# Two homes for the mixture outputs, one GpSimd loop over pairs of blocks, and a second mixture that finishes its chunk pairs one by one

## The chip, the cores and the metric

One Trainium2 chip, one of its cores. The metric is the device time of one execution in microseconds (us), as the median of a few runs.

## The reference

Two layers work on 2048 tokens of width 256 (two sequences of 1024). Each layer is a cross-attention to 154 context rows, and then a mixture of 8 experts of which every token uses its best two:

```python
x = x + attention0(layernorm(x), ctx)          # 16 heads
x = x + mixture0(layernorm(x))                 # silu(x@wg) * (x@wu) @ wd, inner width 1024
x = x + attention1(layernorm(x), ctx, phi)     # one head
x = x + mixture1(layernorm(x))                 # gelu(x@W1a) * (x@W1b) @ W2, inner width 512
# mixture: per token the two largest gate logits, softmax over them as shares;
# mixture1 keeps at most 640 (token, expert) pairs for one expert, the rest is dropped
```

## The kernel before

The program is written by hand, one instruction stream for each engine, with semaphores between them. In each mixture the tokens are first sorted by expert: GpSimd scatters the normalised rows (and two shares, the token's number and the expert, all in one row) into a buffer `rows` in HBM, with a region for each expert. Each region is padded with rows whose token number lies out of range. Then `experts(l)` runs on TensorE, ScalarE and VectorE (l.n is 0 or 1 for the two mixtures). It walks over **blocks** of 256 rows of one expert; a last block of an expert with at most 128 rows is done at half width (`width` P instead of BLK), which I call a half block. Which blocks belong to which expert is read at run time from a small `table` that `count(l)` on VectorE fills.

A number with about 22 bits is carried as two fp16 parts, `hi` and `lo`, so each product takes three matmuls. The inner width is cut into **chunks** of 128 columns and two chunks form a **pair**; the first mixture has 4 pairs for each block, the second has 2. For block g:

- TensorE (`one_block`) computes gate and up of each pair into PSUM banks, transposes block g+1 (`turn_block`), waits until the outputs of block g-1 have left their banks (semaphore `_y`), and then computes the outputs (L685 is the helper `mm` of all matmuls): first all products with `h_hi`, then all with `h_lo`. For the second mixture a full block has 48 matmuls for gate and up, 8 transposes (L933) and 24 for the outputs; a half block has 48 at half the columns, 8, and 12.
- ScalarE computes the activation of the gate (L1267), casts the product to its high part `h_hi` (L1271), starts the load of block g+2 (`load`, L1253, into the one `x_raw`), and at the end waits for the output products and for the semaphore `_added`, and writes the outputs times their share from PSUM to `yb` (L1280).
- VectorE multiplies activation and up (`h32`, L1804), takes the low part `h_lo` (L1809), and in `turned(g+1)` copies the transposed block from PSUM to `xbT` (L1783) and works out its shares and token numbers, `carried` (L1786 to L1790).
- GpSimd (`add_results`) goes over the experts and in each over its blocks. For a block it copies the token numbers to `row_to` (L571), waits for `yb`, issues two indirect DMAs of 128 rows that add `yb` to the sums in HBM (L575), waits until they have landed (L580), and raises `_added`.

There is one `yb`, so the outputs of block g leave PSUM only when the addition of block g-1 has landed; and the ScalarE stream stands at this wait, with the activations of block g+1 behind it. There is one `x_raw`; its next load waits for `carried`, which reads the ends of its rows.

The weights of a coming expert are split beside the blocks: SyncE loads a chunk of 1024 columns, ScalarE makes its high part (`high_part`, L1129) and VectorE its low part (`low_part`, L1405). In the second mixture there are 3 such chunks for each expert, all beside the first block of the expert two before; I call such a block a splitting block. At what step of the block each is done stands in

```python
l.beside     = (([0], [1], [2], [3, 4], [5]), ([0], [1, 2], []))[n]   # ScalarE
l.low_beside = (([0], [1], [2], [3], [4, 5]), ([0], [], [1, 2]))[n]   # VectorE
```

After the first mixture, SyncE waits for `_added` of all blocks and loads the sums as the new x. At the end of the second it waits in the same way, and the program is over when all engines have come to their ends.

## Time and profile before

| | |
|---|---|
| median of 3 runs | 883.97 us (883.52 to 884.15) |
| span of the profiled execution | 889.0 us, 5.0 over the median |
| TensorE matmuls busy | 700.3 us, 79% of the span |
| VectorE / ScalarE / GpSimd busy | 547.8 / 403.1 / 302.8 us |
| mean granted TensorE clock | 0.889 of full speed |
| chain that ended last | TensorE 48%, VectorE 18%, "issue" 11%, ScalarE 9%, GpSimd 5%, DMA 5% |

For the profiled execution the page gives the span from its first to its last instruction and no other time of its own. The profiler records one execution, and all durations below are from it. Times in the rows are us from the start of the span. The clock is a share of full speed (1.00 is 2.4 GHz, 0.50 is 1.2 GHz). "Idle before <-releaser" is how long the engine stood before the instruction and what released it.

### The profile page before, as it was taken

To read this page: it belongs to the slowest core of one execution; us is meant where nothing else is said; L and a number is where in the kernel's file an instruction comes from. 1 tells how busy PE (TensorE), PEld (TensorE's weight loads), DVE (VectorE), ACT (ScalarE), POOL (GpSimd) and SP (SyncE) were. 2 spreads that over 40 slices of the span, in tenths; PEclk is the share of its full clock that TensorE was granted. 3 is DMA by queue.
4 is the path that set the end of the run, shared out by engine and by line. 5 is a ranking of instruction groups with operands and counts; after the bars stand their busy time and mean duration, and the time that the engine had idled before them with its cause. 6 is when DMAs were issued, how large, how long until landed. Compare 5 with 4: busy or idle time off the path is not lost.

```text
span 889.0 us, 19049 instructions
## 1 busy us (share of the span) xinstructions
PE 700.3 (79%) x6278; PEld 550.1 (62%) x6278; DVE 547.8 (62%) x1322; ACT 403.1 (45%) x720; POOL 302.8 (34%) x306
## 2 busy tenths in 40 slices
PE   5476796989564799999999899996862098898981
PEld 4232454555354688888897798895531087777771
DVE  7768576887836545647556656547696446566441
ACT  1135466576513434646545555442552044546331
POOL 7505301416337422222121131232167414334342
PEclk9689799989776799999999999997875599999996
DMA  4562300601524542536344643425022555464332
GB/s 140 118 141 51 59 2 24 180 24 49 153 81 151 185 129 36 165 51 171 78 126 98 170 112 101 107 39 179 25 101 95 174 170 131 115 147 114 63 55 40
DMA packets 68418, 92.24 MB, mean 104 GB/s; under 512 B 14442, under 2 KB 54435, under 8 KB 68348
## 3 DMA queue, kind: packets, MB, share of 16 engines
q1 hardware_dynamic: 41788, 63.37, 24.1%
q0 software_dynamic: 14592, 16.24, 10.6%
q10 hardware_dynamic: 11968, 11.72, 5.3%
q8 instruction: 42, 0.69, 0.3%
q14 instruction: 28, 0.23, 0.1%
HBM read 64.21 MB, written 29.87 MB: 106 GB/s over the span
## 4 chain that ended last, share of the span: by engine, by line
PE 48%; DVE 18%; issue 11%; ACT 9%; POOL 5%; DMA 5%; ACTq 2%; another core or an unknown queue 1%; DVEq 0%; POOLq 0%; SPq 0%
PE ps L685 45%; POOL rows L631 3%; DVE probs L1726 3%; DVE mx L1591 2%; DMA out_x<-keys,row_to 2%; DVE keys L1804 2%; DMA probs<-rows 2%; ACT probs L1189 1%; ACT probs L1271 1%; ACT expo L1186 1%; DVE keys L1783 1%; ACT probs L1267 1%; PE ps L933 1%; DVE stats L1383 1%; ACTq L1252 1%
## 5 line engine op out<-in xcount | busy, mean ns | idle before, releaser
L1804 DVE TENSOR_TENSOR keys<-probs,ps 128x512 f32<-128x512 f32 x122 | 82.8, 687 | 177.3 <-ACT probs L1267 86.3
L685 PE MATMUL ps<-keys,slot 128*128 128x256 f16 (+1 forms) x1440 | 146.5, 263 | 5.4 <-DVE keys L1783 2.7
L685 PE MATMUL ps<-keys,probs 128*128 128x256 f16 (+1 forms) x1488 | 139.5, 255 | 5.1 <-DVE probs L1405 3.7
L685 PEld LDWEIGHTS ps<-keys,slot 128*128 128x128 f16 x1440 | 127.8, 99 | 22.8 <-issue 5.4
L685 PEld LDWEIGHTS ps<-keys,probs 128*128 128x128 f16 x1488 | 124.2, 98 | 19.0 <-issue 7.2
L575 POOL DMA_INDIRECT attended<-keys,row_to x42 | 67.2, 1601 | 166.0 <-ACT keys L1280 142.2
L1267 ACT ACTIVATE probs<-ps 128x512 f32<-128x512 f32 x122 | 71.4, 598 | 65.9 <-PE ps L685 63.7
L1280 ACT ACTIVATE keys<-ps,carried 128x256 f32<-128x256 f32 x80 | 33.5, 470 | 117.9 <-POOLq L580 41.6
L1809 DVE TENSOR_TENSOR probs<-keys,probs 128x512 f16<-128x512 f32 x122 | 83.3, 688 | 3.6 <-ACT probs L1271 1.9
L1271 ACT CAST probs<-keys 128x512 f16<-128x512 f32 x122 | 74.8, 614 | 22.0 <-DVE keys L1804 21.9
L1726 DVE TENSOR_TENSOR probs<-expo,probs 128x512 f16<-128x512 f32 x80 | 61.1, 775 | 34.1 <-ACT probs L1189 28.2
L685 PE MATMUL ps<-slot,probs 128*128 128x256 f16 x636 | 74.8, 273 | 3.7 <-ACT probs L1271 3.0
L685 PE MATMUL ps<-probs 128*128 128x256 f16 x612 | 72.4, 273 | 4.8 <-ACT probs L1271 4.4
L575 POOL DMA_INDIRECT out_x<-keys,row_to x38 | 58.8, 1548 | 45.6 <-ACT keys L1280 36.6
L1186 ACT ACTIVATE expo<-ps 128x512 f32<-128x512 f32 x80 | 48.2, 602 | 52.8 <-PE ps L685 46.9
L685 PEld LDWEIGHTS ps<-slot,probs 128*128 128x128 f16 x636 | 60.0, 98 | 14.4 <-ACT probs L1271 4.2
L685 PEld LDWEIGHTS ps<-probs 128*128 128x128 f16 x612 | 57.5, 98 | 15.8 <-ACT probs L1271 4.5
L571 POOL COPY row_to<-carried 128x2 int32 x40 | 10.1, 252 | 139.0 <-issue 45.5
L933 PE MATMUL ps<-identh,probs 128*128 128x128 f16 x336 | 26.5, 224 | 36.5 <-DMA probs<-rows 36.5
L685 PE MATMUL ps<-penalties,identb 128*128 128x462 bf16 x96 | 34.8, 363 | 22.2 <-DVE queries L1569 9.4
L1189 ACT CAST probs<-expo 128x512 f16<-128x512 f32 x80 | 49.0, 619 | 0.0
L1405 DVE TENSOR_TENSOR probs<-inbox,probs 128x1024 f16<-128x1024 f32 x36 | 43.6, 1221 | 6.1 <-ACT probs L1129 6.0
(285 smaller groups left out, 1145.7 us busy)
## 6 DMA issues: line engine op xcount, KB each, us to landing
inbox<-in_W SPq DMA_DIRECT2D x24, 512.0 KB, 3.9
probs<-rows ACTq DMA_DIRECT2D x44, 260.0 KB
inbox<-in_wg SPq DMA_DIRECT2D x16, 512.0 KB, 5.2
inbox<-in_wu SPq DMA_DIRECT2D x16, 512.0 KB, 3.7
inbox<-in_wd SPq DMA_DIRECT2D x16, 512.0 KB, 4.2
rows<-zeros SPq DMA_DIRECT2D x16, 260.0 KB
x<-in_x SPq DMA_DIRECT2D x4, 512.0 KB, 6.1
q_out<-queries SPq DMA_DIRECT2D x8, 256.0 KB, 2.1
```

The source lines that it names most:

```text
L575: pool.indirect_dma_start(out=l.sums, out_offset=bass.IndirectOffsetOnAxis(ap=row_to[:, hf:hf + 1], axis=0), in_=yb[:, hf, :], in_offset=N ...
L685: return pe.matmul(o, l, r, start=start, stop=stop, **kw)
L933: last = pe.transpose(psh[:, 6, part * BLK + hf * P:part * BLK + (hf + 1) * P], x_raw[:, hf, part * P:(part + 1) * P], identh[:, :])
L1186: act.activation(e_ring[:, u % 4, :], ps[:, 4 + u % 2, :], ACT.Exp, scale=float(DK) ** -0.5).then_inc(S("a0_exp"), 1)
L1189: act.copy(p_hi[:, u - 1, :], e_ring[:, (u - 1) % 4, :]).then_inc(S("a0_phi"), 1)
L1267: act.activation(s_act[:, j % 2, :], ps[:, 2 * (j % 2), :], l.act).then_inc(S(r + "_s"), 1)
L1271: act.copy(h_hi[:, 2 * j - 2:2 * j, :].rearrange("p c t -> p (c t)"), h32[:, (j - 1) % 2, :]).then_inc(S(r + "_hh"), 1)
L1280: ins = act.activation(yb[:, hf, :], ps[:, 4 + hf, 0:D], ACT.Identity, scale=carried[:, bass.ds(g, 1), hf, 0:1].rearrange("p b d -> p (b d)"))
L1405: dve.tensor_tensor(w[:, 1, at:at + CH], stage[:, n % STAGES, :], w[:, 0, at:at + CH], ALU.subtract).then_inc(S(f"w_ready{l.n}"), 1)
L1726: dve.tensor_tensor(p_lo[:, u, :], e_ring[:, u % 4, :], p_hi[:, u, :], ALU.subtract).then_inc(S("a0_plo"), 1)
L1804: dve.tensor_tensor(h32[:, j % 2, :], s_act[:, j % 2, :], ps[:, 2 * (j % 2) + 1, :], ALU.mult).then_inc(S(r + "_h32"), 1)
L1809: dve.tensor_tensor(h_lo[:, 2 * j - 2:2 * j, :].rearrange("p c t -> p (c t)"), h32[:, (j - 1) % 2, :], h_hi[:, 2 * j - 2:2 * j, :].rearran ...
```

## The change

Both mixtures: `yb` becomes an array of its own with two homes, used in turn (g % 2), and `_added` starts at 2 instead of 1, so that the outputs of block g leave PSUM when the addition of block g-2 has landed. GpSimd's two nested loops (experts, and blocks of an expert) become one loop over pairs of blocks, whose number `twos` is a new entry of the table. Additions still land one after the other. Where the number of blocks is odd, the last pair has a block that isn't there; its table entry now points to padding rows, so its token numbers are out of range and nothing is added, but its two DMAs are issued and waited for. ScalarE gives it its `_y`. `count` has five more small operations for this.

Second mixture alone: each pair is finished before the next starts. ScalarE does activation, then waits for the product and casts, and only then the next activation. TensorE does for each pair the products with `h_hi` and then with `h_lo` (`outputs_by_pairs`). VectorE copies the transposed block (`turned_rows`) before the low part of the last pair, together with the ends of the rows (`tail_now`, 4 words each), which frees `x_raw`; the shares follow later (`own_shares`) from `tail_now`. The load of block g+2 waits for this copy instead of `carried`. The three weight chunks are spread: on ScalarE one before the first activation, one after the load of block g+2, one after the outputs; on VectorE one before the first product and two at the end of the block.

```diff
-        row_to = sb("row_to", [P, 2], I32)
+        row_to = sb("row_to", [P, 2, 2], I32)
+        tail_now = sb("tail_now", [P, 2, 4], I32)
...
-        yb, keys_at = part(keys, keys_at, [P, 2, D])
+        yb = sb("yb", [P, 4, D])
...
-            l.beside = (([0], [1], [2], [3, 4], [5]), ([0], [1, 2], []))[n]
+            l.beside = (([0], [1], [2], [3, 4], [5]), ([0], [1], [2]))[n]
...
-                wait_counted(sp, S(l.r + "_added"), total + 1)
+                wait_counted(sp, S(l.r + "_added"), total + 2)
...
+                def rows_of(i, q):
+                    wait_counted(pool, S(r + "_carried"), i * 2 + q + 1)
+                    pool.tensor_copy(row_to[:, q, :], carried[:, bass.ds(i * 2 + q, 1), :, 1]...).then_inc(S(r + "_to"), 1)
+                    wait_counted(pool, S(r + "_to"), i * 2 + q + 1)
+
+                def add(i, q):
+                    wait_counted(pool, S(r + "_y"), i * 2 + q + 2)
...
+                def landed(i, q):
+                    pool.wait_ge(S(r + "_stored"), i * 64 + q * 32 + 32)
                     pool.sem_inc(S(r + "_added"), 1)
+
+                with pool.Fori(0, twos) as i:
+                    rows_of(i, 0)
+                    add(i, 0)
+                    rows_of(i, 1)
+                    landed(i, 0)
+                    add(i, 1)
+                    landed(i, 1)
...
-                with pool.Fori(0, E - 1) as e:
-                    add_results(l, e)
-                add_results(l, E - 1)
+                add_results(l)
...
+                def outputs_by_pairs(g, wh, wl, width):
+                    for j in range(pairs):
+                        pe.wait_ge(S(r + "_hh"), g * pairs + j + 1)
...                        (16 or 8 matmuls for the pair: h_hi by wh and by wl)
+                        pe.wait_ge(S(r + "_h"), g * pairs + j + 3)
...                        (h_lo by wh)
+                    last.then_inc(S(r + "_down"), 1)
...
-                act.sem_inc(S(r + "_added"), 1)
+                act.sem_inc(S(r + "_added"), 2)
...
+                    if l.n:
+                        split(0)
+                        for j in range(pairs):
+                            n = g * pairs + j
+                            act.wait_ge(S(r + "_h32"), n + 1)
+                            act.wait_ge(S(r + "_gu_ps"), n * 2 + 1)
+                            act.activation(s_act[:, j % 2, :], ps[:, 2 * (j % 2), :], l.act).then_inc(S(r + "_s"), 1)
+                            act.wait_ge(S(r + "_h32"), n + 3)
+                            act.copy(h_hi[:, 2 * j:2 * j + 2, :]..., h32[:, j % 2, :]).then_inc(S(r + "_hh"), 1)
+                        act.wait_ge(S(r + "_xbT_ps"), g + 3)
+                        act.wait_ge(S(r + "_raw_free"), g + 2)
+                        load(g + 2)
+                        split(1)
+                        results(g)
+                        split(2)
+                        return
...
-                        ins = act.activation(yb[:, hf, :], ps[:, 4 + hf, 0:D], ACT.Identity,
+                        ins = act.activation(yb[:, bass.ds(g % 2 * 2 + hf, 1), :]..., ps[:, 4 + hf, 0:D], ACT.Identity,
...
+                wait_counted(act, S(r + "_y"), total + 1)
+                act.sem_inc(S(r + "_y"), 1)
...
+                def turned_rows(g):
+                    dve.wait_ge(S(r + "_xbT_ps"), g + 2)
+                    dve.tensor_copy(xbT[:, :, :, :]..., psh[:, 6, :]).then_inc(S(r + "_xbT"), 1)
+                    wait_counted(dve, S(r + "_share"), g + 1)
+                    dve.tensor_copy(tail_now[:, :, :], raw[:, :, TOKEN:TOKEN + 4].bitcast(I32)).then_inc(S(r + "_raw_free"), 1)
...
+                    if l.n:
+                        split(0)
+                        for j in range(pairs):
+                            n = g * pairs + j
+                            dve.wait_ge(S(r + "_s"), n + 1)
+                            dve.wait_ge(S(r + "_gu_ps"), n * 2 + 2)
+                            dve.wait_ge(S(r + "_h"), n + 1)
+                            dve.tensor_tensor(h32[:, j % 2, :], s_act[:, j % 2, :], ps[:, 2 * (j % 2) + 1, :], ALU.mult).then_inc(S(r + "_h32"), 1)
+                            if j == 0:
+                                dve.wait_ge(S(r + "_down"), g + 1)
+                            if j == pairs - 1:
+                                turned_rows(g + 1)
+                            dve.wait_ge(S(r + "_hh"), n + 1)
+                            dve.tensor_tensor(h_lo[:, 2 * j:2 * j + 2, :]..., h32[:, j % 2, :],
+                                              h_hi[:, 2 * j:2 * j + 2, :]..., ALU.subtract).then_inc(S(r + "_h"), 1)
+                        own_shares(g + 1)
+                        split(2)
+                        return
```

## Rows read from the trace of the kernel before

**Rows 1.** Busy time by stretch (windows): first mixture; PE, PEld, DVE, ACT, POOL, clock, DMA.
```profile
293.00:607.00 314.00, 304.58 (x3088) 271.86 (x3088) 181.64 (x300) 157.88 (x257) 76.67 (x67) 0.99 0.43 109
```

**Rows 2.** Timeline of TensorE: start, duration, line, operation, idle before.
```profile
461.71 5.57 PE L685 MATMUL ps<-keys,probs 128*128 128x128 f16 x96
...
711.12 7.26 PE L685 MATMUL ps<-keys,slot 128*128 128x256 f16 x48 [0.87 <-DVE keys L1783]
...
746.99 5.41 PE L685 MATMUL ps<-keys,slot 128*128 128x256 f16 x48
...
752.69 3.07 PE L685 MATMUL ps<-slot,probs 128*128 128x256 f16 x24
755.59 2.84 PE L685 MATMUL ps<-keys,slot 128*128 128x128 f16 x48
...
762.13 5.41 PE L685 MATMUL ps<-keys,probs 128*128 128x256 f16 x48 [0.28 <-DVE keys L1783]
...
772.37 5.41 PE L685 MATMUL ps<-keys,probs 128*128 128x256 f16 x48 [0.51 <-DVE keys L1783]
...
781.58 5.41 PE L685 MATMUL ps<-keys,probs 128*128 128x256 f16 x48
...
870.07 1.72 PE L685 MATMUL ps<-probs 128*128 128x256 f16 x12 [0.26 <-ACT probs L1271]
```

**Rows 3.** Chain that ended last, in order of time: start, duration, piece.
```profile
440.46 15.72 PE ps L685 x144
...
606.80 2.71 DMA attended<-keys,row_to
...
735.86 3.65 DMA out_x<-keys,row_to
```

**Rows 4.** Waits, 709 to 889: who waited for whom, us, times, longest.
```profile
ACT keys L1280 <- POOLq L580: 41.6, 11, 4.4
```

**Rows 5.** Timeline of ScalarE.
```profile
462.14 0.84 ACT L1280 ACTIVATE keys<-ps,carried 128x256 f32<-128x256 f32 x2 [4.58 <-PE ps L685]
...
757.10 0.84 ACT L1280 ACTIVATE keys<-ps,carried 128x256 f32<-128x256 f32 x2 [3.32 <-POOLq L580]
757.83 1.08 ACT L1267 ACTIVATE probs<-ps 128x512 f32<-128x512 f32 x2
759.35 1.22 ACT L1271 CAST probs<-keys 128x512 f16<-128x512 f32 x2 [0.44 <-DVE keys L1804]
...
768.29 1.04 ACT L1129 CAST slot<-inbox 128x1024 f16<-128x1024 f32 x1
...
874.71 0.84 ACT L1280 ACTIVATE keys<-ps,carried 128x256 f32<-128x256 f32 x2 [4.19 <-POOLq L580]
```

**Rows 6.** Timeline of VectorE.
```profile
758.63 1.29 DVE L1804 TENSOR_TENSOR keys<-probs,ps 128x512 f32<-128x512 f32 x2 [3.00 <-PE ps L685]
760.07 1.32 DVE L1809 TENSOR_TENSOR probs<-keys,probs 128x512 f16<-128x512 f32 x2 [0.16 <-ACT probs L1271]
761.32 0.68 DVE L1783 COPY keys<-ps 128x1024 f16<-128x1024 f16 x1
...
769.36 1.23 DVE L1405 TENSOR_TENSOR slot<-inbox,slot 128x1024 f16<-128x1024 f32 x1 [0.19 <-ACT slot L1129]
```

**Rows 7.** Timeline of GpSimd.
```profile
615.75 0.24 POOL L608 TENSOR_SCALAR var_p<-mv_a 128x4 f32<-128x4 f32 x1 [5.57 <-DVE mv_a L1395]
...
740.17 0.19 POOL L571 COPY row_to<-carried 128x2 int32 x1 [2.77 <-DMA out_x<-keys,row_to]
...
843.80 0.19 POOL L571 COPY row_to<-carried 128x2 int32 x1 [3.89 <-issue]
845.03 1.55 POOL L575 DMA_INDIRECT out_x<-keys,row_to  x1 [1.04 <-issue]
...
876.43 1.55 POOL L575 DMA_INDIRECT out_x<-keys,row_to  x1 [1.14 <-ACT keys L1280]
878.29 1.54 POOL L575 DMA_INDIRECT out_x<-keys,row_to  x1 [0.30 <-issue]
```

More of the change, by code:

```diff
@@ L47 @@
 TB_FULL = 64
+TB_TWOS = 72
 CH = 1024
@@ L233, in two_layers @@
         room, at = part(queries, at, [1, E], rows=1)
+        unused, at = part(queries, at, [1, AHEAD], rows=1)
+        padding, at = part(queries, at, [1, 1], rows=1)
+        twos, at = part(queries, at, [1, 1], rows=1)
         xps = [sb("xp", [P, GT, RW], F16), part(penalties, 0, [P, GT, RW], F16)[0]]
@@ L574, in add_results @@
                     for hf in range(2):
                         pool.indirect_dma_start(
-                            out=l.sums, out_offset=bass.IndirectOffsetOnAxis(ap=row_to[:, hf:hf + 1], axis=0),
-                            in_=yb[:, hf, :], in_offset=None, bounds_check=N - 1, oob_is_err=False,
+                            out=l.sums, out_offset=bass.IndirectOffsetOnAxis(ap=row_to[:, q, hf:hf + 1], axis=0),
+                            in_=yb[:, 2 * q + hf, :], in_offset=None, bounds_check=N - 1, oob_is_err=False,
@@ L954, in one_block, with outputs_in_passes @@
                     pe.wait_ge(S(r + "_y"), g + 1)
+                    if l.n:
+                        outputs_by_pairs(g, wh, wl, width)
+                    else:
+                        outputs_in_passes(g, wh, wl, width)
+                def outputs_by_pairs(g, wh, wl, width):
+                    for j in range(pairs):
+                        pe.wait_ge(S(r + "_hh"), g * pairs + j + 1)
+                        for c in (2 * j, 2 * j + 1):
+                            at = l.down_at + c * D
+                            for hf in range(width // P):
+                                o, tk = ps[:, 4 + hf, 0:D], slice(hf * P, (hf + 1) * P)
+                                mm(o, h_hi[:, c, tk], wh[:, at:at + D], c == 0, False)
+                                mm(o, h_hi[:, c, tk], wl[:, at:at + D], False, False)
+                        pe.wait_ge(S(r + "_h"), g * pairs + j + 3)
+                        for c in (2 * j, 2 * j + 1):
+                            at = l.down_at + c * D
+                            for hf in range(width // P):
+                                o, tk = ps[:, 4 + hf, 0:D], slice(hf * P, (hf + 1) * P)
+                                last = mm(o, h_lo[:, c, tk], wh[:, at:at + D], False, c == l.hc - 1)
+                    last.then_inc(S(r + "_down"), 1)
+                def outputs_in_passes(g, wh, wl, width):
                     for c in range(l.hc):
```

59 lines of the change are left out of this document (40 added, 19 removed).

## The prediction

> **What bounds the kernel now.** I read the windows first, to see which stages the change can touch. The first mixture keeps TensorE busy for 304.6 of 314.0 us at a clock of 0.99 [rows 1]: it is bound by its matmuls, and what ScalarE or GpSimd save there is worth nothing. The second mixture is another matter. Its matmuls begin at 711.12 and end at 870.07 + 1.72 = 871.79, so 160.7 us for 19 blocks, of which the timeline of TensorE shows 13 full and 6 half ones [rows 2].
>
> The chain gives the price of a matmul without stalls: 144 take 15.72, 0.109 each [rows 3]. A full block has 72 of them, 7.86, and 8 transposes, which take 752.69 - 746.99 - 48 x 0.109 = 0.46; so 8.3 without a stall. An undisturbed full block took 755.59 - 746.99 = 8.60, and its 24 output matmuls show 3.07 [rows 2]: they stood about 0.3 for the last cast, since 24 x 0.109 is 2.62. A half block took 762.13 - 755.59 = 6.54 [rows 2], though its matmuls need about 2.8 + 0.5 + 1.3 = 4.6. If all blocks were undisturbed, the stage would take 13 x 8.60 + 6 x 6.54 = 151.0. It takes 9.7 more. 1.85 of this is the first block, whose first 48 matmuls show 7.26 instead of 5.41 [rows 2]; that is the half clock at the start and no matter of the change. The other 7.8 lie in blocks that follow a half block (762.13 to 772.37 is 10.24, 1.6 too long) and in second ones of two splitting blocks in a row (772.37 to 781.58 is 9.21, 0.6 too long; there are two such) [rows 2].
>
> The waits say why: ScalarE stood 41.6 us before L1280 for GpSimd's L580, the landing of the block before [rows 4]. In a full block this is covered, because 5.7 us of gate, up and transposes lie between; after a half block it comes through.
>
> **Second mixture, full blocks.** With two homes the outputs leave PSUM when TensorE is done with them. Where ScalarE had only TensorE to wait for, this began 462.14 - 461.71 = 0.43 after the next block's first matmul [rows 2, 5]; in the half block at 755.59 it was 757.10, 1.51 after [rows 2, 5]. The new dynamic index of `yb` costs some register operations; no row shows them, I bound them by 0 and 0.3 and take 0.15, so 0.58. Then the first activation can start 757.83 - 757.10 = 0.73 later, at 1.3, and its product (758.63 - 757.83 = 0.80 later) at 2.1, before the pair's matmuls end at 2.6 [rows 5, 6]. So nothing of a full block's start hangs on ScalarE any more, and the 0.3 before the last outputs goes too, because four `h_lo` matmuls of the first pair now lie before them. I take 8.30 for a full block. The serial order costs nothing here: the first product starts when its matmuls are done, at about 2.8, the cast at 3.5, the second activation 0.5 later at 4.0, when the gate of pair 2 is just ready (36 x 0.109 = 3.9), and the second product would be possible at 4.8, but its matmuls end only at 5.2.
>
> **Splitting blocks.** A high part takes 1.04 and a low part 1.23 [rows 5, 6]. The first one, ahead of the first activation, delays the first product from 2.8 to about 3.5; the second product needs TensorE until 5.4, so it is hidden. But the third high part now comes behind the outputs, in the next block: outputs at 0.75 (held 0.3 by the second high part), high part until 2.55, low part until 3.9, and VectorE does it ahead of the next block's first product. That product starts at 3.8, the second at 5.85 instead of 5.45, and the block ends about 0.25 late. Four blocks are of this kind: 1.0. Two blocks are themselves splitting ones behind a splitting one: high part until 3.55, low part until 5.0, product 4.95, cast 5.65, activation 6.15, product 7.0, cast 7.7, low part 8.4 to 9.1, and 12 matmuls behind the cast end at 9.7, which is 1.4 over 8.3: 2.8 for both. Here the change gives nothing (9.21 before). All 13 full blocks: 13 x 8.30 + 1.0 + 2.8 + 1.85 for the clock = 113.5.
>
> **Half blocks.** Here the chain between ScalarE and VectorE is the bound, not TensorE, and the change makes it serial. Steps from the rows: product to cast 759.35 - 758.63 = 0.72, cast to low part 760.07 - 759.35 = 0.72, one instruction to the next on one engine about 0.5 on ScalarE (1.08 for two activations) and 0.6 on VectorE [rows 5, 6]. New: outputs 0.58, activation 1.31, product 2.11, cast 2.83, activation 3.3, product 4.2 (VectorE does the first low part from 3.55), cast 4.9, low part 5.6 to 6.3, two matmuls: the next block starts at 6.6. In the old order the outputs start 0.9 later, but the two activations, products and casts overlap, and the end was the copy to `xbT` behind the last low part, at 761.32 + 0.68 = 762.00 [rows 6]. The copy now lies in front (about 4.8 to 5.5) and is off the path, and the load of the next block starts some 2 us earlier. The three gains of about 0.9, 0.7 and the DMA wait are eaten by the serial order. I take 6.65 each: 39.9. Bounds: 6.1 if outputs and hops go faster, 7.0 if not.
>
> **Sum of the stage:** 113.5 + 39.9 = 153.4, against 160.7: 7.3 saved.
>
> **The end.** Both mixtures have an odd number of blocks (19 here, 21 in the first: 42 and 38 indirect DMAs), so GpSimd's last pair issues two DMAs for a block that isn't there, and nothing hides them in the second mixture. Before: last matmul T = 871.79, the last two DMAs at 876.43 and 878.29 [rows 7]. The first mixture's last addition, of a half block too, landed 2.71 after the start of its second DMA [rows 3], so 881.0, T + 9.2. After: measured from the start s of the last half block, the outputs of the full block before it are in `yb` at 0.58 + 0.84 = 1.4; the first DMA starts 0.88 later (876.43 - 875.55 [rows 5, 7]), at 2.3, the second 1.86 later [rows 7], and lands 3.65 after its start [rows 3], 7.8. Then the next pair begins: row_to 740.17 - 739.51 = 0.66 later and its first DMA 845.03 - 843.80 = 1.23 after that [rows 3, 7]: 9.7, the second 11.6, landed 14.3. The block that isn't there: 0.88 + 1.86 + 2.71 = 5.45, so 19.7. With s = T - 6.6 this is T + 13.1, 3.9 more than before. That additions no longer hold up the last outputs is worth nothing, because GpSimd itself is later than they are (3.1 against T + 2.2). For the empty DMAs the nearest row is the second half of a half block, whose rows are all padding: 1.54 to issue, and landed in 2.71 [rows 3, 7]. Bounds: 0, if the engine ends don't wait for it, and 6.4, at 3.65 each.
>
> The Trainium skill (DMA: Bandwidth & Descriptors, Anatomy of one DMA) gives a GpSimd DMA a fixed cost of about 2.0 us whatever it carries, mostly the write's receipt. For 128 rows of 1 KB that makes 2.3 us, and the row (3.65 less 1.54 of issuing) agrees with 2.1; for a DMA without rows the trace has only 2.71 - 1.54 = 1.2. By the page the empty one would cost 0.8 more and the kernel would take 881.7.
>
> **First mixture.** No wait for the landing comes through there, so the second home buys nothing. The index costs ScalarE 0.15 for a block, hidden but at the two or three places where its outputs lie on the path: 0.3 lost. The missing block costs GpSimd 5.45 after 609.5, when SyncE has already gone on; GpSimd's next needed work is at 615.75, after 5.57 of idle [rows 7], and its result is needed some 5 us later. Hidden. The five additional operations in `count` (about 0.1 to 0.2 each) run beside GpSimd's scatter, which ends later. Nothing.
>
> **Net:** 7.3 - 3.9 - 0.3 = 3.1 saved. The sum stands against the profiled span of 889.0, which is 5.0 above the median of the runs; I take the difference over to the median: 883.97 - 3.1 = 880.9.
>
> **Rivals.** (a) The half blocks and the second splitting blocks go better than my chain: halves at 6.1 (3.3 saved) and the two at 8.8 (1.8 saved): 876. For it: the hops are partly waits for other things. Against: 0.72 and 0.80 recur all over the timelines. (b) *Slower:* the serial order costs in full blocks as well. One place decides it, the second activation behind the first cast: if the first cast starts after 4.1 instead of 3.5, then each 0.1 beyond delays all 13 full blocks by 0.1. At 0.4 over, with the halves at 7.0, 13 x 0.4 + 6 x 0.35 = 7.3 are lost again, the end stays 3.9 longer and the time is 888; it decides from 0.25 us over on. Half of it, 885, is likelier. (c) The end isn't 3.9 longer, because the empty DMAs come back at once or the program doesn't wait for them: 877 to 878. (d) The double home does not remove the wait: GpSimd becomes the bound, at 1.86 + 3.65 + 0.88 = 6.4 and 1.86 + 3.65 + 1.89 = 7.4 for the two of a pair, 6.9 on average against 153.4 / 19 = 8.1 for a block. Its room is 1.2 us a block, so this is unlikely; if landings took 1.5 longer, nothing would be gained in the stage and the time is 888. (e) Gain and end cancel: 883 to 885.
>
> **How the numbers follow.** Forecast (gain of 6.5 to 8.5 in the stage) 0.42; (a) 0.13; (b) 0.15; (c) 0.08; (d) 0.02; (e) 0.15; the page's longer empty DMA 0.05. A measurement of this kernel tells apart about 0.2%, 1.8 us. Faster: forecast 0.38, (a), (c), the page 0.03: 0.62, less a little of (c): 0.60. Same: (e) and the rims of the forecast: 0.22. Slower: (b), (d) and a part of (e): 0.18. The range leaves out the far halves of (a) and (b): 876.8 to 885.2. For the likeliest case alone it is 879.5 to 882.2.
>
> **What would show it.** Right: no wait of ScalarE for the landing before it writes the outputs; full blocks 8.3 apart; half blocks about 6.6; the two second splitting blocks still over 9; two more indirect DMAs in each mixture (84 in all instead of 80); the last matmul about 7 earlier and the last indirect DMA only 3 to 4 earlier than now. Wrong: full blocks at 8.6 or more with TensorE waiting for a product or cast; half blocks far from 6.6; the last two DMAs missing or much shorter; a lower clock in the second mixture.

## The result, and the profile after

The changed kernel took **889.6 us** (median of 4 runs, 889.13 to 893.25) against 883.75 of the kernel before on the same chip (4 runs): a ratio of 1.0072, 95% interval 1.0049 to 1.0094. Measured again later, beside 14 runs of the kernel before on another chip, it was 1.0065 (1.0044 to 1.0086). Slower by about 6 us, where I had forecast 3.1 us faster; 889.6 also lies outside my range of 876.8 to 885.2.

The table divides the spans of the profiled executions. Each border is the start of a matmul in the timeline of TensorE: the first one of the first mixture, the first one after its outputs, the first gate matmul of the second mixture, and the end of the last matmul. Column 1 is work that the change doesn't touch; it shows by how much executions differ anyway. "Before, again" is a run of the unchanged kernel (described below), "change, again" the second measurement.

| us | up to first mixture | first mixture | between the mixtures | second mixture | its first block | after the last matmul | span |
|---|---|---|---|---|---|---|---|
| before | 295.2 | 306.0 | 109.8 | 160.7 | 11.1 | 17.2 | 889.0 |
| before, again | 292.4 | 305.4 | 108.2 | 161.1 | 10.6 | 17.0 | 884.1 |
| change | 289.2 | 304.1 | 112.5 | 162.0 | 15.1 | 19.6 | 887.4 |
| change, again | 290.6 | 306.6 | 112.0 | 159.6 | 12.0 | 19.7 | 888.5 |

So three things are to be explained: the stage between the mixtures, which I had called unchanged, is longer by about 3 (2.2 to 4.3, whichever two profiles are compared); the second mixture, from which I had expected 7.3, is on average of the two profiles as long as before (162.0 and 159.6 against 160.7 and 161.1); and the end is 2.5 longer (3.9 expected).

The waits of ScalarE in the changed kernel, 709 to 889 (who waited for whom, us, times, longest), answer to [rows 4]:

```profile
ACT probs L1308 <- DVE keys L1891: 42.6, 38, 2.1
...
ACT yb L1337 <- PE ps L700: 25.1, 14, 2.1
```

The 41.6 us of waiting for GpSimd's landing are gone. ScalarE now waits for TensorE before it writes outputs (L1337), and 42.6 us for VectorE's products (L1891) before it casts, which is the new serial order.

The timeline of TensorE of the changed kernel (start, us, line, operation, count, idle before and what ended it) answers to [rows 2]:

```profile
753.44 2.85 PE L700 MATMUL ps<-keys,slot 128*128 128x128 f16 x48
...
756.99 1.10 PE L700 MATMUL ps<-slot,probs 128*128 128x256 f16 x6 [0.25 <-ACT probs L1308]
758.94 1.12 PE L700 MATMUL ps<-slot,probs 128*128 128x256 f16 x6 [0.85 <-ACT probs L1308]
760.19 5.41 PE L700 MATMUL ps<-keys,probs 128*128 128x256 f16 x48
765.44 0.61 PE L948 MATMUL ps<-identh,probs 128*128 128x128 f16 x8
765.89 1.47 PE L700 MATMUL ps<-probs 128*128 128x256 f16 x12
767.83 1.48 PE L700 MATMUL ps<-probs 128*128 128x256 f16 x12 [0.47 <-ACT probs L1308]
...
837.71 5.40 PE L700 MATMUL ps<-keys,probs 128*128 128x256 f16 x48
...
846.01 2.84 PE L700 MATMUL ps<-keys,probs 128*128 128x128 f16 x48
...
852.82 5.41 PE L700 MATMUL ps<-keys,probs 128*128 128x256 f16 x48
...
866.70 1.12 PE L700 MATMUL ps<-probs 128*128 128x256 f16 x6 [0.85 <-ACT probs L1308]
```

A full block now takes 846.01 - 837.71 = 8.30, as predicted, and a half block 852.82 - 846.01 = 6.81 (760.19 - 753.44 = 6.75). In the half block TensorE waits 0.85 between its two groups of six matmuls for the second cast: the two pairs in series. The splitting block that starts at 760.19 takes 9.56 (the next starts at 769.75), and it does show a wait for a cast.

**Between the mixtures.** GpSimd in the changed kernel (its timeline, around the end of the first mixture), to be laid beside [rows 7]:

```profile
599.01 1.55 POOL L582 DMA_INDIRECT attended<-yb,row_to  x1 [0.30 <-issue]
599.98 0.78 POOL L576 COPY row_to<-carried 128x2 int32 x1
602.73 4.48 POOL L582 DMA_INDIRECT attended<-yb,row_to  x1 [1.97 <-issue]
607.52 1.57 POOL L582 DMA_INDIRECT attended<-yb,row_to  x1 [0.31 <-issue]
616.01 0.13 POOL L653 IOTA xp<- 128x4 int32 x1 [6.92 <-DMA attended<-yb,row_to]
...
616.81 1.05 POOL L625 TENSOR_TENSOR ry_a<-var_p,minus_half 128x4 f32<-128x4 f32 x1
```

The real block's second DMA starts at 599.01. The empty block's two follow at 602.73 and 607.52, and GpSimd goes on at 616.01. The chain of the same stretch (start, us, piece) has the two landings:

```profile
599.01 2.71 DMA attended<-yb,row_to
...
607.52 8.19 DMA attended<-yb,row_to
```

The empty block holds GpSimd for 615.71 - 601.72 = 14.0 us, where I had counted 5.45: its first DMA takes 4.48 to issue instead of 1.5, and its second lands after 8.19 instead of 2.71. What else ran at the time is in VectorE's timeline:

```profile
602.30 3.48 DVE L1464 TENSOR_TENSOR slot<-inbox,slot 128x1024 f16<-128x1024 f32 x3
...
617.99 0.19 DVE L1958 COPY lg_x<-ps 128x32 f32<-128x32 f32 x1 [4.78 <-POOL ry_a L625]
```

and in the DMA view of 600 to 616 (busy tenths and GB/s in 40 slices):

```profile
DMA  0001000372999999999999999999999996000000
GB/s 0 0 1 2 0 0 0 108 156 59 320 389 387 381 392 351 351 346 353 341 356 348 346 410 374 389 430 390 369 400 390 451 359 226 11 10 10 21 0 0
```

The slow issue (602.73 to 607.21) begins inside the three low parts of VectorE (602.30 to 605.78) and ends 1.43 after them, about one undisturbed issue. The same trace has this in small in the second mixture: the indirect DMAs of 739.21, 774.18 and 807.12 began inside a single low part, took 2.33, 1.95 and 2.02 us, and each ended 1.41 to 1.42 after that low part, while those that began just before one took 1.54 to 1.60. So the issue is put down to the low parts. The landing coincides with the full DMA engines: the loads of the new x and of weight chunks move 320 to 450 GB/s from 604 to 613, and the empty DMA lands after them. It has no bytes to carry: on the page GpSimd's DMA queue (q0) moves 16.24 MB before and after the change, with 576 packets more, 144 for each of the four empty DMAs. Then VectorE stands 4.78 us for GpSimd's `ry_a`, and TensorE 4.94 for VectorE (here TensorE's timeline, of the same stretch):

```profile
605.88 1.94 PE L1077 MATMUL ps<-ident,x 128*128 128x128 f32 x8 [7.58 <-DMA x<-attended]
...
619.79 4.66 PE L700 MATMUL ps<-heads,qs 128*128 128x162 f32 x16 [4.94 <-DVE expo L1962]
```

The Trainium skill (SBUF — State Buffer, section "SBUF: two separate sides") warns of such a delay for GpSimd's DMAs: while VectorE runs an operation in one of its modes with two ports, of which it names a copy of f32, GpSimd can't write its descriptors. The rows above show the same delay, 4.48 against 1.55 us, but beside subtractions of two SBUF operands, which that note doesn't name; here the measurement decides.

**The first block of the second mixture.** ScalarE (timeline of the changed kernel):

```profile
710.72 1.28 ACT L1167 ACT_TABLE_LOAD   x1 [27.40 <-issue]
712.01 1.05 ACT L1167 CAST probs<-inbox 128x1024 f16<-128x1024 f32 x1
713.08 1.28 ACT L1306 ACT_TABLE_LOAD   x1
714.37 0.60 ACT L1306 ACTIVATE probs<-ps 128x512 f32<-128x512 f32 x1
...
760.72 0.84 ACT L1337 ACTIVATE yb<-ps,carried 128x256 f32 x2 [1.83 <-PE ps L700]
762.18 1.05 ACT L1167 CAST slot<-inbox 128x1024 f16<-128x1024 f32 x1 [0.62 <-issue]
763.13 0.59 ACT L1306 ACTIVATE probs<-ps 128x512 f32<-128x512 f32 x1
```

The high part that now comes first brings a load of ScalarE's activation table of its own, and the activation behind it a second one: 1.28 + 1.05 + 1.28 us before the first activation, where a single table load of 1.28 stood before. The rows of 760.72 to 763.13 are for the splitting block; I come back to them.

**The end.** GpSimd again, after the last matmul (866.70 + 1.12 = 867.82), for [rows 7]:

```profile
870.87 1.55 POOL L582 DMA_INDIRECT out_x<-yb,row_to  x1 [1.04 <-issue]
872.72 1.54 POOL L582 DMA_INDIRECT out_x<-yb,row_to  x1 [0.30 <-issue]
873.71 0.76 POOL L576 COPY row_to<-carried 128x2 int32 x1
876.41 1.55 POOL L582 DMA_INDIRECT out_x<-yb,row_to  x1 [1.94 <-issue]
878.26 1.54 POOL L582 DMA_INDIRECT out_x<-yb,row_to  x1 [0.31 <-issue]
```

The empty block's two DMAs start 5.54 after those of the real one (876.41 - 870.87 and 878.26 - 872.72). The page counts 84 indirect DMAs in the two mixtures (80 before), the four predicted.

### The profile page after: what moved, and what is told of

Same layout as the page of the kernel before. It is cut to its first block, busy times and chain, and to the rows that moved or that the text cites. A ratio compares the mean times of both kernels' runs of the same rounds, so it can differ in the third digit from the quotient of the medians.

```text
span 887.4 us, 18969 instructions
## 1 busy us (share of the span) xinstructions
PE 699.9 (79%) x6278; PEld 554.0 (62%) x6278; DVE 552.5 (62%) x1352; ACT 405.3 (46%) x721; POOL 314.5 (35%) x311
## 3 DMA queue, kind: packets, MB, share of 16 engines
q0 software_dynamic: 15168, 16.24, 10.4%
## 4 chain that ended last, share of the span: by engine, by line
PE 49%; DVE 19%; issue 10%; ACT 8%; DMA 5%; POOL 4%; ACTq 2%; SPq 1%; DVEq 1%; POOLq 0%
PE ps L700 47%; DVE probs L1791 3%; POOL rows L646 2%; DVE mx L1650 2%; ACT probs L1227 1%; ACT probs L1306 1%; DMA attended<-yb,row_to 1%; PE ps L948 1%; DVE keys L1891 1%; ACT expo L1224 1%; DVE stats L1442 1%; DMA out_x<-yb,row_to 1%; DVE keys L1859 1%; DMA x<-in_x 1%; ACT xln L1174 1%
## 5 line engine op out<-in xcount | busy, mean ns | idle before, releaser
L582 POOL DMA_INDIRECT attended<-yb,row_to x44 | 71.6, 1627 | 211.6 <-ACT yb L1337 199.5
L1908 DVE TENSOR_TENSOR keys<-probs,ps 128x512 f32<-128x512 f32 x84 | 57.6, 688 | 110.3 <-ACT probs L1321 56.5
L582 POOL DMA_INDIRECT out_x<-yb,row_to x40 | 64.6, 1614 | 70.3 <-ACT yb L1337 47.1
L700 PE MATMUL ps<-slot,probs 128*128 128x256 f16 x636 | 76.8, 276 | 8.8 <-ACT probs L1308 8.0
L1321 ACT ACTIVATE probs<-ps 128x512 f32<-128x512 f32 x84 | 49.7, 597 | 49.7 <-PE ps L700 49.2
L1337 ACT ACTIVATE yb<-ps,carried 128x256 f32 x80 | 33.4, 469 | 83.6 <-PE ps L700 62.9
L1913 DVE TENSOR_TENSOR probs<-keys,probs 128x512 f16<-128x512 f32 x84 | 57.6, 686 | 1.5 <-ACT probs L1325 0.3
L1325 ACT CAST probs<-keys 128x512 f16<-128x512 f32 x84 | 51.6, 614 | 12.8 <-DVE keys L1908 12.7
L576 POOL COPY row_to<-carried 128x2 int32 x42 | 24.2, 577 | 67.4 <-DMA out_x<-yb,row_to 28.0
```

The source lines that it names most:

```text
L582: pool.indirect_dma_start(out=l.sums, out_offset=bass.IndirectOffsetOnAxis(ap=row_to[:, q, hf:hf + 1], axis=0), in_=yb[:, 2 * q + hf, :], ...
L700: return pe.matmul(o, l, r, start=start, stop=stop, **kw)
L1321: act.activation(s_act[:, j % 2, :], ps[:, 2 * (j % 2), :], l.act).then_inc(S(r + "_s"), 1)
L1325: act.copy(h_hi[:, 2 * j - 2:2 * j, :].rearrange("p c t -> p (c t)"), h32[:, (j - 1) % 2, :]).then_inc(S(r + "_hh"), 1)
L1337: ins = act.activation(yb[:, bass.ds(g % 2 * 2 + hf, 1), :].rearrange("p b d -> p (b d)"), ps[:, 4 + hf, 0:D], ACT.Identity, scale=carried ...
L1908: dve.tensor_tensor(h32[:, j % 2, :], s_act[:, j % 2, :], ps[:, 2 * (j % 2) + 1, :], ALU.mult).then_inc(S(r + "_h32"), 1)
```

## Experiments

All are ratios to runs of the kernel before on the same chip, with 95% intervals. The stage names are those of the table above.

**1. How much do executions differ?** The kernel before, unchanged.

> The kernel before, unchanged, for a second profile. The first profile spans 889.0 us where its runs took 884, the profile of the changed kernel 887.4 where its runs took 889.6, so the two traces can't be subtracted as wholes. Expected: a span near 882, with the extra 6 to 7 us of the first profile lying before the first mixture (its first block at about 289 instead of 295), and the two mixtures and the second attention as in the first profile within 0.5 us: first mixture 306 or less from its first block to its last matmul, 109.8 from there to the first block of the second mixture, 160.7 for that mixture, 17.2 from its last matmul to the end.

It took 885.8 us, with a span of 884.1, and only 2.9 of the extra of the first profile lay in the start. The second mixture and the end repeated within 0.4 us (161.1 and 17.0), the stage between the mixtures within 1.6 (108.2), the start within 2.9. Differences of a single stage under about 2 us between two profiles are therefore weak evidence; the second mixture's later blocks and the end repeated best.

**2. No empty block in the first mixture.** The loop runs over whole pairs and an odd last block is done behind it, in the first mixture only.

```diff
+                if l.n in (0,):
+                    total = pool.value_load(table[l.n][0:1, 8:9], min_val=1, max_val=MAXBLK)
                 with pool.Fori(0, twos) as i:
...
+                if l.n in (0,):
+                    with pool.If(total - twos * 2):
+                        rows_of(twos, 0)
+                        add(twos, 0)
+                        landed(twos, 0)
...        (and in count, twos holds the number of whole pairs for this mixture)
```

> The changed kernel, but in the first mixture GpSimd's loop runs over whole pairs only and the odd last block is done in a branch of its own, so nothing is issued for a block that isn't there; in the second mixture the empty block stays. Theory 1 (the empty block holds GpSimd until 615.8, and through it the first exponentials of the second attention): TensorE's wait there falls from 4.9 to about 1.1 and the kernel takes 3.8 less, 885.8. Rival (the empty block is hidden there, as I predicted, and the lost time comes from the order inside the pairs): 889.6 within 0.8.

Ratio 1.0003 (0.998 to 1.0026), 12 runs: most of the loss is gone, as by theory 1. The stage between the mixtures took 105.7. GpSimd's and TensorE's timelines of this kernel, in this order of fences, at the same place:

```profile
605.76 0.14 POOL L660 IOTA xp<- 128x4 int32 x1 [1.33 <-DMA attended<-yb,row_to]
...
612.04 1.06 POOL L632 TENSOR_TENSOR ry_a<-var_p,minus_half 128x4 f32<-128x4 f32 x1
```

```profile
609.75 1.94 PE L1084 MATMUL ps<-ident,x 128*128 128x128 f32 x8 [7.58 <-DMA x<-attended]
...
618.73 2.44 PE L707 MATMUL ps<-heads,qs 128*128 128x162 f32 x16 [1.15 <-ACT qs L1389]
```

From the first transposes of x to the matmuls with `qs` it is 618.73 - 609.75 = 8.98, against 619.79 - 605.88 = 13.91 in the change: 4.9 us, with the same TensorE work. This pair of profiles is at the upper end: over all twelve of this document the stretch takes 8.97 to 10.37 in the seven without this empty block and 12.56 to 13.91 in the five with it, and the whole stage 105.7 to 109.8 against 112.0 to 113.0, on average 4.9 more. That is the price of the first mixture's empty block.

**3. No empty block in either mixture.** The same edit with `(0, 1)`.

> The same in both mixtures: no empty block at all. Theory 1: on top of the 3.8, the end loses its 5.5 us (0.9 to the first empty DMA, 1.9 to the second, 2.7 to its landing): 880.3, faster than the kernel before. Rival (something else sets the end, so that the last empty DMAs are hidden): 885.8 as without the empty block in the first mixture alone.

Ratio 0.9963 (0.9936 to 0.9991), 12 runs, by the ratios 3.5 us under experiment 2, where 5.5 were expected; the end took 15.6 instead of 19.6. The last two of GpSimd's DMAs in its timeline start 3.14 and 4.99 after the last matmul (859.91 + 1.12 = 861.03), and nothing follows:

```profile
864.17 1.55 POOL L582 DMA_INDIRECT out_x<-yb,row_to  x1 [1.02 <-issue]
866.02 1.54 POOL L582 DMA_INDIRECT out_x<-yb,row_to  x1 [0.30 <-issue]
```

So the second empty block costs 4.0, and the new order itself makes the end 1.4 to 1.6 shorter (15.6 against 17.0 and 17.2).

**4. The first weight part behind the first activation.** The whole change, with ScalarE's and VectorE's first part of a coming expert's weights behind the first activation and the first product.

```diff
                     if l.n:
-                        split(0)
                         for j in range(pairs):
...
                             act.activation(s_act[:, j % 2, :], ps[:, 2 * (j % 2), :], l.act).then_inc(S(r + "_s"), 1)
+                            if j == 0:
+                                split(0)
...        (and in the same way for VectorE, behind its first product)
```

> The changed kernel with both empty blocks, but in the second mixture the first high part comes behind the first activation and the first low part behind the first product, instead of ahead of them. Theory 1 (the weight part ahead of the activation costs the time that the double home had won): the first block falls from 15.1 to about 10.5, because the activation no longer waits behind the load of the weights and because the engine's activation table is loaded once instead of twice; the splitting blocks after a half block fall from 9.6 to 8.4 (two) and from 8.7 to 8.4 (one), the second of two splitting blocks from 9.6 to 8.6 (two). Sum 9.3: 880.3. Rival (the serial order of activation, product and cast is what costs, wherever the weight parts stand): the splitting blocks stay within 0.3, the first block gains its 1.3 of table load alone: 888.3.

Ratio 1.0017 (0.9993 to 1.004), 12 runs, about 5 per mille under the whole change: between the two cases, since I had expected 9.3 us and some 4.5 came. The first block took 10.6, as expected, but experiment 10 will show that some 3 us of the change's 15.1 belonged to one execution. The second mixture took 154.5, near the 153.4 that I had predicted for the change. TensorE's timeline at the block that took 9.56 in the change:

```profile
756.71 5.41 PE L700 MATMUL ps<-keys,probs 128*128 128x256 f16 x48
761.96 0.61 PE L948 MATMUL ps<-identh,probs 128*128 128x128 f16 x8
762.40 2.78 PE L700 MATMUL ps<-probs 128*128 128x256 f16 x24
765.42 5.41 PE L700 MATMUL ps<-keys,probs 128*128 128x256 f16 x48 [0.23 <-issue]
```

It now takes 765.42 - 756.71 = 8.71, and the 24 output matmuls run in one piece of 2.78, without the wait of 0.47 for the second cast.

**5. Both: no empty block, and the first weight part late.**

> No empty block in either mixture, and the first weight part of an expert behind the first activation and product instead of ahead of them. Theory (the loss is the sum of three separate costs, the empty block of the first mixture, the longer first block of the second mixture, and the longer end, and the mixture's own order is a gain): the first block takes about 10.6 us, the mixture about 154.5, the end about 15.6, the stage between the mixtures about 108, and the time is 8 to 10 us under the kernel before, ratio 0.989 to 0.991. Rival (the two removals overlap, since both free the same stretch of ScalarE and VectorE near the mixture's start, or the mixture's gain is taken back by a later start): no better than without the empty block alone, ratio 0.995 to 0.997.

877.0 us against 885.2, ratio 0.992 (0.9888 to 0.9952), 6 runs: 0.8% **faster** than the kernel before. The theory's 0.989 to 0.991 lies inside the interval, and the rival's 0.995 just inside too, so these runs alone don't decide between them. Between the mixtures 107.9, the end 15.6, both as expected; the second mixture took 156.7, 1.2 of the missing 2.2 in its first block (11.75), where the transposes of the second block waited 1.06 for their rows.

**6. The homes and the pair loop alone.** The second mixture keeps the old order and spread of the weights; the two homes, the pair loop with both empty blocks and the additions to `count` stay.

```diff
-            l.beside = (([0], [1], [2], [3, 4], [5]), ([0], [1], [2]))[n]
+            l.beside = (([0], [1], [2], [3, 4], [5]), ([0], [1, 2], []))[n]
...
-                    if l.n:
+                    if False:
                         outputs_by_pairs(g, wh, wl, width)
...        (and in the same way for the order on ScalarE and VectorE)
```

> Of the change only the two homes, the loop over pairs of blocks and the table's additions; the second mixture keeps the old order and the old spread of the weight parts. Theory: both empty blocks stay, so the stage between the mixtures is 3 to 5 us longer than before and the end 2 to 3; the homes give back only the wait of the output evictions in full blocks, about 0.25 us a block in some places, 1 to 2 us in all. Ratio 1.003 to 1.007. Rival (the homes are what makes the second mixture shorter, by 4 us or more, and the order within a block gives nothing): the mixture takes under 157 us and the ratio is 0.998 to 1.002.

Ratio 1.0096 (1.0064 to 1.0128), 6 runs, worse than the theory's 1.003 to 1.007. Between the mixtures 112.7 and at the end 21.1, so the two empty blocks cost their 4 to 5 and 4; the second mixture took 159.7, about 1.2 less than before. The waits of ScalarE, 709 to 889:

```profile
ACT yb L1337 <- issue: 43.1, 14, 3.8
...
ACT yb L1337 <- POOLq L589: 17.6, 5, 3.7
```

The landing still holds up some outputs (17.6 us; 41.6 and 34.9 in the two profiles before), and little is won in blocks: in the old order the load of the coming rows starts late too, and TensorE stood 0.73 for it in the half block of this kernel:

```profile
758.05 0.62 PE L948 MATMUL ps<-identh,probs 128*128 128x128 f16 x8 [0.73 <-DMA probs<-rows]
```

**7. The order alone.** The new order and spread of the second mixture on the one old `yb`, with the old block-by-block additions.

```diff
-        yb = sb("yb", [P, 4, D])
+        yb, keys_at = part(keys, keys_at, [P, 2, D])
...
-                act.sem_inc(S(r + "_added"), 2)
+                act.sem_inc(S(r + "_added"), 1)
...        (add_results and its two nested loops as before the change)
```

> Of the change only the second mixture's order, the spread of its weight parts and the table's additions, on the one home and with the old loop that adds block by block. Theory: no empty block, so the stage between the mixtures is at most 1 us longer and the end as before; the first block takes 13 to 15 us, half blocks 6.75 to 6.85; full blocks gain less than in the whole change where the outputs' eviction waits for the addition before it. The mixture takes 159 to 163 us; ratio 0.999 to 1.004. Rival (the order needs the second home: with one home the eviction, now the last step on ScalarE of a block, waits for the landing of the block before): blocks of 9 us and more everywhere, the mixture 166 us or more, ratio over 1.005.

Ratio 1.0092 (1.006 to 1.0125), 7 runs: the rival's case. The second mixture took 172.7, 11 to 12 longer than before, while the end (15.7) and the stage between the mixtures (108.7) were those of kernels without an empty block. ScalarE's timeline in a half block and behind it:

```profile
748.16 0.39 ACTq L1281 DMA_DIRECT2D probs<-rows  x1
753.09 0.84 ACT L1327 ACTIVATE keys<-ps,carried 128x256 f32<-128x256 f32 x2 [5.79 <-POOLq L585]
753.82 0.60 ACT L1296 ACTIVATE probs<-ps 128x512 f32<-128x512 f32 x1
```

and the chain there:

```profile
746.94 5.89 DMA out_x<-keys,row_to
```

The outputs wait 5.79 us for the landing of the addition before, and the half block's first activation stands behind them in the stream; with the two pairs in series, TensorE can't make up for it. Part of the 12 us is its clock: behind four of the half blocks, in which TensorE had stood up to 2.3 us at a time, the 48 matmuls for gate and up show 6.92, 6.16, 7.46 and 6.34 us at a granted clock of 0.77, 0.88, 0.72 and 0.85, where 5.41 at 1.00 is usual: 5.2 us in all. (Both the GpSimd copies and the landings were also longer here: 5.89, against 3.65 in [rows 3].) So order and homes are no two gains that add up. Homes alone: about 1.2 less in the second mixture. Order alone: 11.8 more. Together, on average of two profiles, nothing (1.1 more and 1.3 less), and 6.4 less with the late first part.

**8. The paddings.** The whole change, but the second load of rows waits only for the paddings of the first two experts.

```diff
                 clear(0, l.r + "_padded_first")
-                with sp.Fori(1, E) as e:
+                clear(1, l.r + "_padded_second")
+                with sp.Fori(2, E) as e:
...
-                act.wait_ge(S(r + "_padded"), 16 * (E - 1))
+                act.wait_ge(S(r + "_padded_second"), 16)
                 load(1)
...        (the rest of the paddings is waited for before load(g + 2); in both mixtures)
```

> The whole change, but the second load of rows waits only for the padding of the experts 0 and 1; the rest of the paddings is waited for before the third load. Theory (the first block is long because the second load starts 2.4 us later behind the landing of the last padding, and ScalarE does the first weight part and both table loads behind it): the second load starts 2 to 5 us earlier, and the first block takes 10.5 to 13 us instead of 15.1; ratio 0.995 to 0.998 against the whole change's 1.007 gives about 1.003 here. Rival (what holds the first block is the weights' landing or ScalarE's own order, not the padding): 14.5 to 15.1 us, ratio 1.006 to 1.009 as for the whole change.

Ratio 1.0025 (1.0003 to 1.0048), 12 runs, and the first block took 11.5. That looks like the theory, but experiment 10 takes the support of the block away: the whole change itself had a first block of 11.95 in its second profile. The ratio is 4 to 5 per mille under that of the change, and the intervals of 1.0025 and 1.0065 just overlap; what made the difference stays open. The profile is of the slowest of the 12 runs (892.45), and its end took 21.3, because the addition before the last one landed after 5.21 us and not 3.61 as in the change: the end too differs between executions.

**9. Everything: both of experiment 5, and the early padding.**

> No empty block, the first weight part behind the first activation, and the second load of rows waits only for the paddings of the experts 0 and 1. Theory (in the kernel with the first two of these the second load still waits for the last padding's landing and its own landing stands before the transposes of the second block, with an idle TensorE of 1.06 us there): the load starts about 2 us earlier and the first block takes 10.4 to 11.0 us instead of 11.75; the mixture about 155.5 to 156, ratio 0.989 to 0.992, 0.5 to 1.5 us under the kernel without the early padding (877.0 us, ratio 0.992). Rival (the idle time before the transposes only moves to the wait for the first activation, since the second load can't start before the first block's rows are copied out): first block 11.5 us or more, same time as without.

878.6 us against 884.6, ratio 0.9934 (0.9913 to 0.9955), 6 runs. The first block was 10.8, as the theory has it, and in it TensorE's transposes no longer waited for rows; but the time is that of experiment 5 (0.992), and two later blocks (7.56 and 9.56 us, where the kernel of experiment 5 took 6.98 and 8.71) were longer. TensorE's timeline shows how:

```profile
750.03 0.62 PE L956 MATMUL ps<-identh,probs 128*128 128x128 f16 x8 [2.05 <-DMA probs<-rows]
...
752.69 6.28 PE L708 MATMUL ps<-keys,probs 128*128 128x256 f16 x48
```

It stood 2.05 us for its rows (1.50 in the same block of experiment 5), and the granted clock was then 0.63 over the outputs and 0.86 over the next 48 matmuls, 6.28 instead of 5.41. The early padding is not worth anything that these runs can show. Why these rows came late stays open.

**10. The change again, on the same chip as experiment 9.** The kernel is that of the change, without an edit.

> The whole change again, beside the run above and the kernel before on one chip. If the parts add up (first empty block 4 to 5 us, first block of the second mixture 4, the end 2.5, against a gain of about 6 in the mixture's other blocks): ratio 1.004 to 1.008, stage between the mixtures 112 to 113, first block 14.5 to 15.5, end 19 to 21.5. If the first comparison was high by its few runs: ratio 1.000 to 1.003, with one of these three near the value of the kernel before.

Ratio 1.0065 (1.0044 to 1.0086), 9 runs: the sum of the parts, not the accident of few runs. Between the mixtures 112.0, the end 19.7; only the first block, at 11.95, is under what I expected. Where the two profiles of the change differ is seen in the chain before that block, first the earlier profile, then the later one:

```profile
703.95 4.51 DMA rows<-zeros
```

```profile
707.26 2.50 DMA rows<-zeros
```

The last padding landed after 4.51 us in the one and after 2.50 in the other, with the second load, both table loads and the first high part behind it. In the first profile TensorE then stood 3.01 us, and its granted clock was 0.62 over the stretch of output matmuls that followed (24 in 4.42 us, where 24 at full clock take 2.78, so part of it at 1.2 GHz); in the second it stood 0.18 and the clock was 1.00, that is 2.4 GHz, over the same matmuls. So of the 15.1 us, some 3 belong to that one execution.

## Why the prediction was wrong

Between the forecast and the profiles lie 8.7 us (3.1 faster forecast, 5.6 slower by the stages of the two pairs of profiles): 7.2 of them in the second mixture and 3.2 in the stage between the mixtures, less 1.4 because the end cost less than forecast and 0.3 because the first mixture cost nothing.

**The step that failed first in time: "First mixture ... Hidden."** I charged the first mixture's empty block with 5.45 us and held it against GpSimd's next needed work, 5.57 of idle and "some 5 us" more. The cover was about right (14.0 spent and 4.9 lost leave 9.1 that were hidden); the price was not. 5.45 was built from rows of a quiet stretch ([rows 3, 7]), and here it was 14.0: 3.0 more for the issue beside VectorE's low parts, 5.5 more for a landing behind loads at 320 to 450 GB/s, and 0.1 ahead of them. Experiment 2 shows the cost, 4.9 us in the profiles, and by the ratios 1.0065 to 1.0003, about 5.5 us. That it is the low parts and the loads which stretch it is read from rows that coincide (for the low parts in four places of the trace), and wasn't tested by moving either. No rival named this place; my slower ones were the serial order (b) and GpSimd as the bound (d). The second didn't come about, as ScalarE waits for no landing. The first didn't in plain full blocks, which take 8.30, but it did in the splitting blocks that follow here.

**The step that failed in the second mixture, the larger miss: splitting blocks, "so it is hidden."** I let the first high part delay the first product from 2.8 to 3.5 us after the block's start and found slack for the rest of the chain. In the block at 760.19 ScalarE starts the high part only at 762.18, with 0.62 of "issue" after the outputs (the change of expert), and the product came at 764.40, so 4.2; product to cast 0.7, activation 0.5, product 0.8, cast 0.7, matmul 0.7 brought the second pair's outputs to 7.64, beyond the 7.2 at which TensorE was ready. The first cast started at 4.9, past the 4.1 that my rival (b) gives as its condition. Of the three splitting blocks behind a half block (8.3 forecast) two took 9.6 to 9.9 and one 8.7 to 8.8. With the edit of experiment 4 they took 8.7 to 8.8 and 8.32. The two second ones of a pair of splitting blocks were as forecast: 9.5 to 9.7, against 9.7. Over the stage the sum of my error is 6.2 us in the second profile: 1.8 in the first block, 3.7 in the other full ones, 0.7 in the halves.

**The first block, "1.85 for the clock" and nothing else.** I put the part ahead of the activation in the general rule and didn't see that in the first block nothing precedes it: there it costs its own 1.05, and a second table load of 1.28 with it. Without both ahead of the activation (experiment 4) the block took 10.6, 1.4 less than in the second profile of the change and 0.4 over my 10.15. I had also called the operations added to `count` nothing. They are on the chain: SyncE's paddings wait for the table, and the second load waits for the paddings. In the changed kernel `count` ran from 685.79 to 690.55, 4.8 us, about 0.6 more than before.

**Half blocks:** 6.7 to 6.8 for 6.65, within the bounds; 0.7 us in all. Outputs started 0.53 after a block's first matmul (760.72 - 760.19), where I had 0.58: the new index costs 0.10 over the 0.43 of before, and the 0.15 that no row bore out was near.

**The end:** forecast from the chain to the last landing, T + 13.1. The last DMA started at 878.26, T + 10.4, and T + 13.1 is 2.71 later as forecast. But the term was 2.4 to 2.7 instead of 3.9. The spans end 8.0 us after the last landing that I work out in this way for the kernel before (17.2 - 9.2) and 7.9 in experiment 3, but 6.4 in the change (19.6 - 13.15); I had taken this stretch to be the same. The empty block added 4.0 to the span and 5.45 to GpSimd's chain; this 1.5 is no accident: the stretch is 7.8 to 8.0 in all six profiles whose last block is a real one and 6.4 to 6.5 in all six with an empty one. One difference stands in the code, that SyncE's wait for `_added` counts real blocks only, so that GpSimd alone is late for an empty one; whether this is the reason no run shows. The rival (c), that it costs nothing, is out.

**The net:** by the stages of the table, on average, +3.2 between the mixtures, +2.5 at the end and -0.1 in the second mixture make 5.6, and the two ratios give 6.4 and 5.8. The gain I had forecast in the second mixture can be had, but not by this change: with the first weight part moved the stage takes 6.4 us less than before in experiment 4, 4.2 and 3.8 less in experiments 5 and 9, and with the empty blocks gone as well the kernel is 0.8% faster than before (experiment 5, the best kernel of this study).

## What to carry to other kernels

An operation that does nothing still costs its issue and its landing, and its neighbours can stretch both (14.0 us here, where a quiet stretch gave 5.45): price it with rows from the stretch in which it will stand, not from a quiet one, and rather branch around it. Before a loop's step is moved to the front of the body, look at the first round by itself: what it hides behind in the steady state isn't there yet. And test the parts of a change both alone and together: here the order without the second home costs 12 us, the home without the order gives 1, and neither number tells what they do together.

## What the runs showed of the hardware that was not expected

- GpSimd's indirect DMA of 128 rows took 4.48 us to issue (4.49 in the second profile) while VectorE ran three subtractions of 128x1024 f32 into f16, and 1.55 without them. Begun inside a single one it took 1.95 to 2.33 and ended 1.41 to 1.42 after it.
- An indirect DMA all of whose rows are out of range still has 144 packets. It landed 1.2 us after its issue ended in a quiet stretch and 6.6 us (607.52 + 8.19 - 609.09) beside loads that filled the DMA engines.
- A plain cast as the first instruction of ScalarE's loop brought a table load of 1.28 us, and the activation after it another one. With the activation first, there was one alone.
- The landing of the same padding DMA was 4.51 us in one execution and 2.50 in another, and the 2 us came back as 3.1 in the block behind it, because TensorE stood 3.01 us and worked on at a clock of 0.62.
